# Which engine issues the weight transfers: half of the staged tiles go to ScalarE's DMA queue, the memory and output strips to SyncE's

## What is computed

```python
x = x + 0.5 * ffn(layernorm(x))
x = x + attn(layernorm(x))
x = x + 0.5 * ffn(layernorm(x))

def attn(h):                       # causal linear attention in chunks of 128, plus a fixed memory
    q, k, v = h @ w_q.T, h @ w_k.T, h @ w_v.T
    sq, sk = elu(q) + 1, elu(k) + 1
    memory_output = (sq @ memory) / clip(sq @ memory_norm)
    local_output = causal(sq, sk, v)           # state S += sk.T @ v from chunk to chunk
    out = g * memory_output + (1 - g) * local_output
    return out @ w_o.T

def ffn(x):                        # a global net on the mean over tokens, then 3 cycles
    gf = sigmoid(mlp_g(mean(x)))
    for _ in range(3):
        tf = sigmoid(mlp_c(x))     # 1024 -> 1024 -> 512 -> 256 -> 1, gelu between
        x = x + coupling(gf, tf) * twist(x)
```

## Time and profile before

| what | us |
|---|---|
| three runs: lowest, median, highest | 4996.77, 5080.83, 5193.49 |
| the profiled execution, its own time | 5007.59 |
| span of its slowest core (core 3) | 5006.1 |
| spans of the eight cores | 4950.9 to 5006.1 |

### The profile page before, as it was taken

One profiled execution on the slowest core, in us unless ns is written; L12 is line 12 of the kernel. 1 busy time (PEld: TensorE's weight loads), 2 busy tenths in 40 slices (PEclk: granted clock), 3 DMA queues, 4 the chain that ended last, 5 costly groups with the idle time before them and its releaser, 6 DMA issues. The chain is left out here.

```text
span 5006.1 us, 34731 instructions; the slowest of 8 cores (4950.9 to 5006.1 us)
## 1 busy us (share of the span) xinstructions
PE 2692.2 (54%) x10855; PEld 1122.5 (22%) x10855; DVE 1705.8 (34%) x2399; ACT 1256.6 (25%) x1457; POOL 222.2 (4%) x203
## 2 busy tenths in 40 slices
PE   1120565564656456857856865823156457457365
PEld 1010122121212113313322322310012222222222
DVE  3332333333242322432322322335333432432423
ACT  1211233333323222022132122111023223133131
POOL 0000000000000011111111111100000000000000
PEclk8555778787878778988988988965578777678687
DMA  3454101001000211321321331231210010100000
GB/s 128 157 172 143 63 1 65 3 1 67 1 34 1 88 34 40 93 69 36 90 77 30 89 84 30 71 102 67 72 67 1 21 46 0 58 10 1 34 1 34
DMA packets 358786, 272.80 MB, mean 54 GB/s; under 512 B 271541, under 2 KB 273617, under 8 KB 358610
## 3 DMA queue, kind: packets, MB, share of 16 engines
q1 hardware_dynamic: 213970, 205.56, 13.0%
q10 hardware_dynamic: 144640, 65.03, 4.9%
HBM read 192.96 MB, written 77.59 MB: 54 GB/s over the span
## 5 line engine op out<-in xcount | busy, mean ns | idle before, releaser
L206 PE MATMUL p4pH<-p4xnp,p4cw 128*128 128x512 bf16 x1536 | 405.7, 433 | 155.3 <-ACT p4xnp L97 87.0
L206 PE MATMUL p1pH<-p1xnp,p1cw 128*128 128x512 bf16 x1536 | 400.9, 428 | 159.8 <-ACT p1xnp L97 87.3
L206 PEld LDWEIGHTS p4pH<-p4xnp,p4cw 128*128 128x128 bf16 x1536 | 164.0, 108 | 400.8 <-issue 281.3
L206 PEld LDWEIGHTS p1pH<-p1xnp,p1cw 128*128 128x128 bf16 x1536 | 162.4, 107 | 403.0 <-issue 266.6
L206 PE MATMUL ptr<-idf,x0t 128*128 128x128 f32 x256 | 58.5, 402 | 337.1 <-DVE stg L97 181.5
L97 DVE TENSOR_SCALAR p4crow<-row,c 1x512 bf16<-1x512 f32 x24 | 12.8, 534 | 651.2 <-ACT row L97 651.2
L206 PE MATMUL pA_<-xn_p,wq_strip 128*128 128x512 bf16 x512 | 136.2, 417 | 169.5 <-DVE xn_p L97 108.3
L97 DVE TENSOR_SCALAR p1crow<-row,c 1x512 bf16<-1x512 f32 x24 | 12.8, 533 | 617.9 <-ACT row L97 617.9
L206 PE MATMUL p4pG<-p4h,p4cw 128*128 128x512 bf16 (+1 forms) x816 | 190.2, 388 | 57.2 <-ACT p4h L97 57.2
L206 PE MATMUL p1pG<-p1h,p1cw 128*128 128x512 bf16 (+1 forms) x816 | 183.8, 379 | 57.5 <-ACT p1h L97 57.5
L97 DVE CAST v_bf<-pB_ 128x512 bf16<-128x512 f32 x64 | 44.3, 692 | 490.8 <-PE pB_ L206 490.8
(11 more groups left out here) (218 smaller groups left out, 4362.2 us busy)
## 6 DMA issues: line engine op xcount, KB each, us to landing
x_sb<-x2f SPq DMA_DIRECT2D x12, 2048.0 KB, 9.0
x0t<-hs SPq DMA_DIRECT2D x8, 2048.0 KB, 16.0
x0f<-stg SPq DMA_DIRECT2D x8, 2048.0 KB, 9.2
x_sb<-x1f SPq DMA_DIRECT2D x8, 2048.0 KB, 9.2
wq_strip<-awq SPq DMA_DIRECT2D x64, 256.0 KB, 3.1
wk_strip<-awk SPq DMA_DIRECT2D x64, 256.0 KB, 3.0
wq_strip<-awm ACTq DMA_DIRECT2D x64, 256.0 KB, 3.2
wo_strip<-awo ACTq DMA_DIRECT2D x64, 256.0 KB, 3.5
```

Of the source, the lines that this page charges most:

```text
L206: i = getattr(e, name)(*a, **kw)
```

## The change

Two things change, and no computing instruction. In `emit_weight_load` the tiles of slot 1 are issued on ScalarE (GS(blk) is blk.scalar), those of slot 0 stay on SyncE. In `emit_pb` and `emit_wo` the memory strips and the wo strips are issued on SyncE, where ScalarE did it before. The waits ahead of each issue stay what they were.

```diff
@@ emit_weight_load
-                    @blk.sync
+                    ldq = blk.sync if slot == 0 else GS(blk)
+
+                    @ldq
                     def _(q, kt=kt, c0=c0, cw=cw, slot=slot, free_at=free_at,
                           sw=sw):
                         if free_at is not None:
@@ emit_pb
-                        @blk.scalar
-                        def _(s, et=et, msl=msl, msem=msem):
-                            wm_slot[msl].wait(s)
-                            s.dma_start(
+                        @blk.sync
+                        def _(q, et=et, msl=msl, msem=msem):
+                            wm_slot[msl].wait(q)
+                            q.dma_start(
                                 out=mem_strip[:, msl, :, :],
@@ emit_wo
-                        @blk.scalar
-                        def _(s, b=b, ft=ft, wsl=wsl, swo=swo):
-                            wo_slot[wsl].wait(s)
-                            s.dma_start(
+                        @blk.sync
+                        def _(q, b=b, ft=ft, wsl=wsl, swo=swo):
+                            wo_slot[wsl].wait(q)
+                            q.dma_start(
                                 out=wo_strip[:, wsl, :, :],
```

## The result

| | before | changed |
|---|---|---|
| median of all runs | 4998.95 us (10 runs) | 5067.6 us (9 runs) |
| ratio | 1 | 1.0128, 95% interval 1.0114 to 1.0141 |
| profiled execution | 5007.6 us | 5067.6 us |
| span of the slowest core | 5006.1 us | 5066.1 us |

The change costs 1.28%, 64 us of 4999. The forecast was 5062 us in a range of 5025 to 5140, with 0.86 for "within 2%"; the loss is within 2% but far outside the 0.14% that the measurement leaves open.

What follows compares the result with a forecast made beforehand. No engine bounds the whole span; TensorE, busiest at 54%, waits now for one engine, now another. Terms 66.2 + 8 - 13.8 - 6.3 = +54.1 us on the profiled 5007.6 us gave 5062 us, range 5025 to 5140.

Steps and rivals of the forecast that it cites:

- The seam: P2, from emit_wo of even blocks to the next emit_pb: TensorE waits for a memory strip, 66.2 us over four seams.
- The cold start: After each of four seam waits in P2, TensorE's first matmuls run at half pace: 2.0 us each, 8 us.
- rival D: P2's odd passes: the clock stays down for a whole pass after each wait, 108 us more, 5170 us; chance 0.06.
- B: P2 seams: strip not held behind 2 MB load, lands 4.2 us from issue; waits 45.9 us, 5041 us; chance 0.08.
- C: P2 seams: queue worse than one load, strip landing 15.6 us, 5.9 us more at four seams, 5086 us; chance 0.11.
- What the move gives back: P2's odd passes: strips 3 to 8 no longer share DMA engines with store and load, 13.8 us less.
- The wo strips: emit_wo in P2: moving these strips to SP changes nothing, 0 us, with bounds of 17 us either way.
- near 50: P2: TensorE's total waits for wo strips were expected to stay near 50 us.
- The weight prologues: Starts of P0, p1, P3, p4: tile pace stays, SP reaches the x load earlier, 6.3 us less in all.
- The sum: Whole kernel: seam waits, cold starts, odd-pass gain and prologue gain together, +54.1 us.
- The chances: Whole kernel, taking about 2% as what a measurement can tell: faster 0.02, same 0.86, slower 0.12.

## Why the prediction was right, and where not

The seam, its place and its mechanism: right. The forecast of 18.9 us three times and 9.5 once, 66.2 us, met 18.37, 18.13, 18.48 and 10.70, 65.7 us. At the fourth seam 1.2 us were missing: the store took 8.1 us there and not 7.4, the strip landed 1.24 us behind it and not 1.05, and TensorE started 0.45 us after the landing, which my sum left out at every seam. The experiments show both halves, the load's place (the load moved behind the memory strips) and the store's (the store moved there too).

The cold start: 8 us forecast. The first steps after the waits (from 2071.47 to 2077.68, for one) take 6.2 to 6.5 us instead of 4.0: 9.6 us in all. Right in kind, 1.6 us short: a wait costs 2.2 to 2.5 us. (The prediction calls 2.9 us the likeliest case and yet adds up 2.0.) The clock came back within a step or two, and rival D fell. B and C fell with the waits, which came to within 1.2 us of the forecast at every seam. B's 4.2 us is the median of two strips of the kernel before, one issued at 2055.43 beside the store that took 5.4 us, and one issued at 2059.43, half a us ahead of the load, that took 3.0; the next, issued at 2065.55 while the load was under way, took 4.6, so the value was fair though its row did not show what it was read for. On SP's queue the first strip behind a load took 9.3 to 10.1 us, at all three seams of all eight cores.

What the move gives back: -13.8 us forecast, -13.0 us measured on the slowest core (what is left of the four passes without wait and cold start, 129.6 us against 142.6), on the eight cores -6.7 to -15.1 us. On the slowest core 65.7 + 9.6 - 13.0 makes up the 62.2 us by which the passes grew, but for rounding.

The wo strips: 0 us, right for the changed kernel (162.4 against 162.1 us), though the waits for them fell from 50.3 to 41.3 us on the slowest core, where "near 50" was forecast. Moved alone they cost 17 us in the passes, through an early fetch that I didn't see; only the order of the changed kernel hides it. The work of bounding an issue's move stopped at what waits for it, and left out that it may come earlier than before and meet another transfer.

The weight prologues: this term failed. I took off 6.3 us, since SP reaches the x load earlier. It did so by 0.8 us instead of 3.4 in p1: the tiles on two queues came a little slower (the cast that frees SP's last slot was over 50.5 us after the first issue, before 47.9), and the first cast of x then started 13.7 us after the load's issue instead of 11.9. The measured effect is +0.7 us in p1 by the cores' median. My working took the time of one slot's cast from one trace as if it were fixed, and didn't let the load's own landing change.

The sum came out at +54 us; measured are +64 by the ratio, and +60 between the two profiles on the slowest core. The prologues, forecast at -6.3 and measured at about nothing, are 6 to 7 us of the difference, and the odd passes 2 (60.4 forecast, 62.2 measured). P2 outside the odd passes adds -1.3 to +5.5 us by core, and p4 differs by more than that in both directions; what moves these is open. The forecast time of 5062 us lies nearer to 5067.6 than this suggests, because it started from the profiled execution's 5007.6, 9 us above the median before.

The chances: here the prediction failed outright. It said that a measurement tells about 2% from no change, and so gave 0.86 to "the same" while its own sum was +1.1%. The ratio's interval is 0.27% wide; a loss of 1.3% is plainly told. The step that failed is that bound of 2%, not the mechanism: what the runs show in its place is a ratio of 1.0128 with an interval of 1.0114 to 1.0141, so that a loss of 0.14% could have been told. With a forecast range of its own of 5040 to 5090, all of it above the time before, the text should have said that the kernel gets slower.

## What to carry to other kernels

An issuing engine's queue is a program in order, waits included: before a transfer is moved to another engine, list what now stands ahead of it there, and whether that waits for something later than the transfer's own condition; a prefetch behind a store that waits for the end of the step is no prefetch. Look also at what the moved transfer may now do too early. Where loads through a few slots set the pace, more slots help (1.7 to 1.1 us a tile here) and a second queue does not (by the ratio of 0.999 with two slots; with four by one profile and one time).

## What was not expected of the hardware

Behind a 2 MB load a strip landed about 1 us after the load. Behind a 2 MB store it was much the same. The issues of 3278 to 3284 us in the changed kernel, with the us to landing last:

```profile
x2f<-x_sb SPq DMA_DIRECT2D x1, 2048.0 KB, 8.1
wq_strip<-awm SPq DMA_DIRECT2D x2, 256.0 KB, 9.1
```

The first strip, issued 0.45 us behind the store, took 8.9 us and so landed 1.24 us after it (1.23 to 1.24 on all eight cores). The store itself took 8.0 to 8.1 us there on every core, and 6.8 to 7.5 at blocks 0 to 5, where nothing was issued behind it until it had landed. And with four tiles of 256 KB in flight one came every 1.1 us, on one queue as on two, while each took 4.0 to 4.2 us to land instead of 2.9.
